# Attention rows ahead of a head's loads, a later wait on TensorE, and an earlier gelu table in a vision transformer layer

## The chip, the cores and the metric

The kernel runs on one core of one Trainium2 chip. The metric is the device time of one execution in microseconds (us). A core has five engines that run side by side and meet at semaphores: TensorE (PE, matrix products), VectorE (DVE), ScalarE (ACT, functions such as exp and gelu), GpSimd (POOL) and SyncE (SP, which only issues transfers here). Each runs its own instructions in order. Products of PE land in PSUM, a memory of eight banks (0 to 7); transfers (DMA) move data between the large memory and the working memory.

## The reference, cut to what matters

```python
h = tok_embed(x)                      # 4 images 224x224, patches of 4: 3137 tokens of 128 features each
h = h + attn(layernorm(h))            # 8 heads of 16, softmax over all 3137 keys
h = h + ffn(layernorm(h))

# attn, for each image and head
attn = softmax(q @ k.T * scale + pos_bias)   # pos_bias from a table of 32 distance buckets
out  = (attn @ v) ... @ Wo

# ffn, for each image
aw     = softmax(x @ attn_w + attn_b)        # over the tokens
pooled = sum(x * aw)                         # one vector
gates  = softmax(pooled @ gate_w + gate_b)   # 8 experts, the best 2 are taken, g is normalised
eo     = gelu(gelu(x @ w1[e] + b1[e]) @ w2[e] + b2[e])   # 128 -> 512 -> 128
y      = g[e1] * eo[e1] + g[e2] * eo[e2]
```

All of it is in float32.

## The kernel before, in words

Tokens lie along the free dimension, features along the 128 partitions. An image (batch b of 4) is cut into 8 chunks of 393 columns (W). There are three parts. The first (to about 212 us) embeds the patches, normalises and computes q, k and v for all images; these go out to the large memory. The second is attention: 32 heads (NBH = 4 x 8), one after the other, and within each head two passes, each over 25 tiles of 128 keys and 4 chunks of queries. The third, from about 2496 us on, is the MLP of the experts.

**Attention.** A unit is one tile of 128 keys by one chunk of queries. `fast_order` puts three units in a group (two where a guest comes in). For a group PE computes scores into three PSUM banks (`scores`, lines 666 and 669), in turn banks 0 to 2 and 3 to 5; ACT takes the exponential of the whole group in one instruction (line 843); POOL multiplies the units near the diagonal by a bias (line 925); PE multiplies by the values four units at a time into banks 6 and 7 (`values`, line 748). PE runs `AHEAD` = 2 groups ahead of ACT. After a pass (25 batches of four units) DVE drains banks 6 and 7 (`drain`, lines 1002 to 1013; the semaphore `s_o` counts the drained passes), normalises, and SP stores the half head to `att_rows` (`store_half`, line 469). A head's q, k and v pieces are eleven transfers (`load_head`, lines 446 and 458), two heads ahead of their use, into the buffers of the head that was just drained, so SP waits for `s_o` first.

**Guests.** While the heads of image b+1 run, PE visits 33 guest matmuls that finish image b's attention and prepare its MLP (`guest_order`, `visit`, line 696): Y multiplies the attention rows of a chunk by Wo, M, V and S are mean, variance and pool scores, G the gates. Three are placed in each pass from the second on, at units 35, 58 and 80 of 100. The one that this text speaks of most, Y4 (the Y of chunk 4), is the second of the fifth pass of a stage; a stage is the 16 passes of one image. The attention rows of chunk c lie in one of four slots, c % 4 of the tile `att`, which shares its memory with `halves` (so a profile calls the load `halves<-att_rows`). Chunks 0 to 3 are loaded at the end of the stage before (line 574), chunks 4 and 5 in the loop of the second head of the stage, 6 and 7 in that of the third. Each `load_attention` first waits until the guest that used the slot before is received (Y0 for chunk 4). The 33 guests of the last image come in the MLP, after unit 3 and each further unit (`LATE`), into bank 6 (`LATE_PS`), one of the two banks that the drain reads.

**SP's order.** SP works through one list in order; for head n: store the first half (which waits for its normalisation), wait until head n's two passes are drained, issue the eleven pieces of head n+2, then the attention rows where there are any, then store the second half.

**The MLP.** A unit U is one chunk and one expert: four products of 128 by 393 into banks 0 to 3 (`experts`, line 712), gelu on ACT (line 861), four products accumulated in bank 4 or 5 (line 720) for the unit before, gelu again (line 868), and DVE adds it to the result (line 1130). Every product is two passes of float32 in the trace (x8 for four products). ACT holds one table of functions at a time; exp and gelu are in different ones, and the builder puts a table load before the first instruction that needs another.

Of the kernel before, what the change touches and what calls it, by code (L numbers as in the profile page):

```python
# [13 lines left out]
ACT = mybir.ActivationFunctionType  # L14
AX_X = mybir.AxisListType.X

P = 128
# [43 lines left out]
def at(count):  # L61

    return count + 1
# [52 lines left out]
def build(nc, B, S, d):  # L116
    T, W, TP, KT = sizes(B, S)
    LAST = T - (KT - 1) * P
    NBH = B * HEADS
# [24 lines left out]
    with top:  # L144
        def sbuf(ctx, name, shape, dt=F32):
            return ctx.enter_context(nc.sbuf_tensor(name, shape, dt))

        def semaphore(ctx, name):
            return ctx.enter_context(nc.semaphore(name))

        held = ExitStack()
# [4 lines left out]
        def primed(ctx, name=None, start=1):  # L156

            s = semaphore(ctx, name) if ctx else spare.pop()  # L160
            to_prime.append((s, start))
            return s
# [9 lines left out]
        eps_t = sbuf(top, "eps_t", [P, 1])  # L172
# [5 lines left out]
        ctx = ExitStack()  # L178
        with ctx:
# [117 lines left out]
            gate_b = sbuf(ctx, "gate_b", [P, E])  # L297
            iota8 = sbuf(ctx, "iota8", [P, 2, E])
            root = sbuf(ctx, "root", [P, 3, W])
            st = sbuf(ctx, "st", [P, B, 16])  # L300
            pooled = sbuf(ctx, "pooled", [P, P])
            gt = sbuf(ctx, "gt", [P, B, 8, E])
# [27 lines left out]
            s_o = primed(held, "f_o")  # L330
# [5 lines left out]
            s_o_out = [primed(held, f"f_o_out{i}") for i in range(2)]  # L336

            s_w3 = semaphore(held, "f_w3")
            s_set3 = semaphore(held, "f_set3")
            s_att = [semaphore(held, f"f_att{i}") for i in range(4)]  # L340
            s_guest_mm = semaphore(held, "f_guest_mm")
# [39 lines left out]
            def guest_number(b, kind, c):  # L381

                return b * GUESTS + guest_list.index((kind, c))

            def expert_unit(U):

                return U // NU, U % NU // 2, U % 2

            LATE = {3 + i: (B - 1) * GUESTS + i for i in range(4 * CH)}
# [47 lines left out]
            def _(sp):  # L437
# [24 lines left out]
                def load_head(n):  # L462
                    for i in range(PIECES):
                        load_piece(n, i)

                def store_half(n, side):
                    sp.wait_ge(s_norm_o, 2 * n + side + 1)
                    dst = bass.AP(att_rows, n * (CH * 32 * W) + side * (4 * 32 * W), [[W, P], [1, W]])
                    sp.dma_start(dst, o_norm[:, side]).then_inc(s_o_out[side], 16)
# [55 lines left out]
                def load_attention(b, c):  # L525

                    if c >= 4:
                        sp.wait_ge(s_guest, guest_number(b, "Y", c - 4) + 1)
                    elif b > 0:
                        sp.wait_ge(s_guest, guest_number(b - 1, "Y", c + 4) + 1)  # L530
                    head = CH * 32 * W
                    src = bass.AP(att_rows, b * (HEADS * head) + c * 32 * W, [[head, HEADS], [W, HD], [1, W]])
                    sp.dma_start(att[:, c % 4], src).then_inc(s_att[c % 4], 16)
# [12 lines left out]
                def load_ln(b):  # L546

                    sp.wait_ge(s_ln2_out[b], 16)
                    sp.dma_start(ln2[b], ln2_rows.ap()[b]).then_inc(s_ln2_in[b], 16)

                for n in range(NBH):
                    b, into = n // HEADS - 1, n % HEADS
                    store_half(n, 0)
                    if n + 2 < NBH:
                        sp.wait_ge(s_o, at(2 * n + 2))
                        load_head(n + 2)
                    if b >= 0 and into == 1:
                        load_attention(b, 4)
                        load_attention(b, 5)
                    if b >= 0 and into == 2:  # L560
                        load_attention(b, 6)
                        load_attention(b, 7)
                    if b >= 0 and into == 6:
                        sp.wait_ge(s_ln2, (b + 1) * CH)
                        sp.dma_start(ln2_rows.ap()[b], ln[:]).then_inc(s_ln2_out[b], 16)
                    if n == NBH - 1:
                        sp.wait_ge(s_pooled, B - 1)
                        sp.wait_ge(s_ln2_out[B - 2], 16)
                        load_ln(0)
                        load_experts(0)  # L570
                    store_half(n, 1)
                    if into == HEADS - 1:
                        for side in range(2):
                            sp.wait_ge(s_o_out[side], at(16 * (n + 1)))
                        for c in range(4):
                            load_attention(b + 1, c)
# [12 lines left out]
            def _(pe):  # L589
# [108 lines left out]
                def experts(U):  # L698

                    if U < B * NU:  # L700
                        b, c, e = expert_unit(U)
                        if U % NU == 0:
                            pe.wait_ge(s_ew[b], EW)
                            if b < B - 1:
                                pe.wait_ge(s_ln2_in[b], 16)
                            else:
                                pe.wait_ge(s_ln2, B * CH)
                        for half in range(2):
                            pe.wait_ge(s_hid, at(max(2 * U + half - 1, 0)))
                            for i in range(2):  # L710
                                sl = 2 * half + i
                                last = nc.tensor.matmul(ps[:, HID_PS + sl, 0:W], w1[b % 2][:, e, sl * P:(sl + 1) * P],  # L712
                                                        ln2[b][:, c * W:(c + 1) * W], start=True, stop=True)
                            last.then_inc(s_hid_mm, 1)
                    if U >= 1:
                        b, c, e = expert_unit(U - 1)
                        pe.wait_ge(s_hid, at(2 * U))
                        pe.wait_ge(s_eo, at(max(U - 2, 0)))
                        for sl in range(HS):
                            last = nc.tensor.matmul(ps[:, EO_PS + U % 2, 0:W], w2[b % 2][:, e, sl], hid[:, (U - 1) % 2, sl],  # L720
                                                    start=(sl == 0), stop=(sl == HS - 1))
                        last.then_inc(s_eo_mm, 1)
# [46 lines left out]
                while done < NB:  # L769
                    values(done)  # L770
                    done += 1
                pe.wait_ge(s_o, at(2 * NBH))
                pe.wait_ge(s_exp, NG)
                pe.wait_ge(s_guest, (B - 1) * GUESTS)
                for U in range(B * NU + 1):
                    experts(U)
                    if U in LATE:
                        visit(LATE[U], LATE_PS)

            @blk.scalar  # L780
            def _(act):
# [48 lines left out]
                def gate_exp(b):  # L830

                    act.wait_ge(s_lg, b + 1)
                    nc.scalar.activation(gt[:, b, 1], gt[:, b, 0], ACT.Exp, bias=st[:, b, 6:7], accum_out=st[:, b, 7:8]).then_inc(s_ge, 1)
# [3 lines left out]
                for g in range(NG):  # L837
# [9 lines left out]
                    if g in gate_exp_at:  # L847
                        gate_exp(gate_exp_at[g])

                for U in range(B * NU + 1):  # L850
                    if U < B * NU:
                        b, c, e = expert_unit(U)
                        if U % NU == 0:
                            act.wait_ge(s_ew[b], EW)
                        if U >= 2:
                            act.wait_ge(s_eo_mm, U - 1)
                        for half in range(2):
                            act.wait_ge(s_hid_mm, 2 * U + half + 1)
                            for i in range(2):
                                sl = 2 * half + i  # L860
                                last = nc.scalar.activation(hid[:, U % 2, sl], ps[:, HID_PS + sl, 0:W], ACT.Gelu,  # L861
                                                            bias=b1[:, 2 * (b % 2) + e, sl:sl + 1])
                            last.then_inc(s_hid, 1)
                    if U >= 1:
                        b, c, e = expert_unit(U - 1)
                        act.wait_ge(s_eo_mm, U)
                        act.wait_ge(s_acc, at(max(U - 2, 0)))
                        nc.scalar.activation(eo[:, (U - 1) % 2], ps[:, EO_PS + U % 2, 0:W], ACT.Gelu,  # L868
                                             bias=b2[:, 2 * (b % 2) + e:2 * (b % 2) + e + 1]).then_inc(s_eo, 1)
                    if U == LATE_EXP:  # L870
                        pool_exp(B - 1)
                    if U == LATE_GEXP:
                        gate_exp(B - 1)
# [267 lines left out]
        ctx = ExitStack()  # L1141
        with ctx:
# [76 lines left out]
            s_o = [primed(ctx, f"s_o{i}") for i in range(2)]  # L1219
# [394 lines left out]
        ctx = ExitStack()  # L1614
# [442 lines left out]
```

## Time and profile before

| | us |
|---|---|
| median of three runs | 2893.42 (2885.08 to 2893.7) |
| the profiled execution, its own time | 2888.52 |
| its span in the trace | 2886.8 |
| ACT busy | 2564.7 (89%) |
| PE busy | 2550.3 (88%) |
| exponentials of line 843, busy / idle before | 2247.2 / 36.0 |

The span is that of the instructions in the trace, and some 1.7 us of the execution's own time lie around it. PE's busy time counts overlapping matmuls once; its share near ACT's doesn't make it a second bound. Idle time of an engine is put down to what ended it.

### The profile page before, as it was taken

The page shows a single profiled execution, that of the slowest core. Times are in us where ns is not written, and L with a number is a line of the kernel's source. Part 1 is how long each engine was busy: PE and PEld are TensorE (multiplying, and loading weights), DVE is VectorE, ACT ScalarE, POOL GpSimd, SP SyncE. Part 2 cuts the span into 40 slices and gives each one's busy share as a digit, 9 for nine tenths or more (in the row PEclk, how much of TensorE's full clock was granted, in tenths as well). Part 3 has the DMA queues.
Part 4 walks back from the last instruction along what each step waited for, and adds up shares of the span by engine and source line. Part 5 has one row for each costly group of instructions (what it writes and reads, how often), then busy time and mean ns, then how long its engine had stood idle before and what let it go on. Part 6 is the DMA issues. An engine that isn't in the chain of part 4 may idle for free.

```text
span 2886.8 us, 121986 instructions
## 1 busy us (share of the span) xinstructions
PE 2550.3 (88%) x55860; PEld 1222.1 (42%) x55860; DVE 846.4 (29%) x1246; ACT 2564.7 (89%) x2732; POOL 785.5 (27%) x1424
## 2 busy tenths in 40 slices
PE   7988888888898999888989998889899988899997
PEld 3443333333343444433434444334344443455554
DVE  5751111111113333211233342112333421244410
ACT  4769999999998999999989999999899999744553
POOL 2113333333323333333333333332333333100000
PEclk9989999999999999999999999999999999999999
DMA  5540111010011110011111100111110000301010
GB/s 136 178 163 11 33 35 31 31 31 30 30 40 34 30 32 30 29 48 32 40 34 32 32 29 29 50 33 37 34 32 31 29 29 31 118 28 32 17 34 19
DMA packets 65896, 125.29 MB, mean 43 GB/s; under 512 B 10034, under 2 KB 55180, under 8 KB 63892
## 3 DMA queue, kind: packets, MB, share of 16 engines
q1 hardware_dynamic: 63324, 110.93, 12.2%
q8 instruction: 444, 7.27, 1.1%
q0 software_dynamic: 2048, 6.43, 0.6%
q14 instruction: 80, 0.66, 0.1%
HBM read 67.30 MB, written 51.30 MB: 41 GB/s over the span
## 4 chain that ended last, share of the span: by engine, by line
ACT 49%; PE 25%; issue 19%; DMA 4%; DVE 1%; SPq 1%; POOL 1%; ACTq 0%; POOLq 0%
ACT shared L843 48%; PE ps L712 6%; PE ps L720 6%; PE ps L748 5%; PE ps L669 3%; PE ps L666 2%; DMA halves<-att_rows 2%; PE ps L696 1%; DMA k_halves<-halves 1%; DVE std L964 1%; POOL ln L911 1%; DMA ln_rows<-ln 0%; PE ps L610 0%; SPq L458 0%; DMA band_rows<-band_sb 0%
## 5 line engine op out<-in xcount | busy, mean ns | idle before, releaser
L843 ACT ACTIVATE shared<-ps 128x1179 f32<-128x1179 f32 x2167 | 2247.2, 1297 | 36.0 <-PE ps L666 28.3
L748 PE MATMUL ps<-shared,va 64*32 64x393 f32 x25600 | 1577.2, 500 | 1.8 <-issue 1.1
L925 POOL TENSOR_TENSOR shared<-shared,e_all 128x310 f32<-128x310 f32 (+19 forms) x1344 | 727.4, 554 | 1571.5 <-ACT shared L843 1565.0
L669 PE MATMUL ps<-qa,ka 48*32 48x393 f16 (+2 forms) x15200 | 728.5, 319 | 149.3 <-ACT shared L843 148.3
L666 PE MATMUL ps<-qa,ka 51*32 51x393 f16 (+8 forms) x13184 | 659.2, 315 | 104.2 <-ACT shared L843 103.7
L748 PEld LDWEIGHTS ps<-shared,va 64*32 64x32 f32 x25600 | 620.8, 139 | 32.7 <-issue 6.6
L669 PEld LDWEIGHTS ps<-qa,ka 48*32 48x32 f16 x15200 | 230.5, 90 | 630.5 <-ACT shared L843 618.4
L666 PEld LDWEIGHTS ps<-qa,ka 51*32 51x32 f16 x13184 | 208.0, 89 | 662.4 <-ACT shared L843 653.4
L1002 DVE COPY xc<-ps 128x393 f32<-128x393 f32 x64 | 36.4, 569 | 1105.5 <-PE ps L748 1105.5
L861 ACT ACTIVATE qa<-ps,b 128x393 f32<-128x393 f32 x256 | 136.4, 586 | 82.2 <-PE ps L712 82.2
L1010 DVE RECIPROCAL sq<-sq 128x393 f32<-128x393 f32 x64 | 167.3, 2615 | 2.2
L868 ACT ACTIVATE ka<-ps,b 128x393 f32<-128x393 f32 x64 | 37.8, 590 | 98.3 <-PE ps L720 98.3
L930 POOL DMA_DIRECT2D out<-h_all x32 | 17.9, 560 | 354.8 <-DVE h_all L1130 354.8
L1130 DVE SCALAR_TENSOR_TENSOR h_all<-ka,gsc,h_all 128x393 f32<-128x393 f32 x64 | 40.2, 628 | 243.3 <-ACT ka L868 243.3
L964 DVE RECIPROCAL std<-std 128x393 f32<-128x393 f32 x32 | 83.7, 2615 | 32.5 <-ACT std L790 32.5
L720 PE MATMUL ps<-qa,v_sb 128*128 128x393 f32 x256 | 89.9, 493 | 0.0
L720 PE MATMUL ps<-qa,e_all 128*128 128x393 f32 x256 | 89.7, 493 | 0.0
L712 PE MATMUL ps<-shared,e_all 128*128 128x393 f32 x256 | 89.7, 493 | 0.0
L911 POOL TENSOR_TENSOR ln<-xc,std 128x393 f32<-128x393 f32 x32 | 32.6, 1017 | 156.4 <-DVE std L964 123.1
L800 ACT ACTIVATE qk_sq<-ps 128x786 bf16<-128x786 f32 x32 | 26.4, 826 | 51.1 <-PE ps L610 28.6
L1022 DVE TENSOR_TENSOR h_all<-h_all,ps 128x393 f32<-128x393 f32 x32 | 18.0, 563 | 162.4 <-PE ps L696 162.4
L720 PEld LDWEIGHTS ps<-qa,e_all 128*128 128x128 f32 x256 | 48.6, 190 | 36.1
(141 smaller groups left out, 1344.8 us busy)
## 6 DMA issues: line engine op xcount, KB each, us to landing
qa<-q_halves SPq DMA_DIRECT2D x64, 196.5 KB
ka<-k_halves SPq DMA_DIRECT2D x64, 196.5 KB
att_rows<-std SPq DMA_DIRECT2D x64, 196.5 KB, 3.2
v_rows<-v_sb SPq DMA_DIRECT2D x4, 1600.0 KB, 6.8
va<-v_rows SPq DMA_DIRECT2D x32, 200.0 KB, 16.0
ln_rows<-ln SPq DMA_DIRECT2D x32, 196.5 KB, 5.7
q_halves<-halves SPq DMA_DIRECT2D x32, 196.5 KB, 3.0
k_halves<-halves SPq DMA_DIRECT2D x32, 196.5 KB, 4.4
```

The lines of the kernel that those rows point to most:

```text
L666: last = nc.tensor.matmul(out[x:y, 0:cut], ka[r:r + 51, par, k0 + x:k0 + y], qa[r:r + 51, par, q0:q0 + cut], start=True, stop=True, tile_p ...
L669: last = nc.tensor.matmul(out[x:y, cut:W], ka[r:r + 48, par, k0 + x:k0 + y], qa[r:r + 48, par, q0 + cut:q0 + W], start=True, stop=True, ti ...
L712: last = nc.tensor.matmul(ps[:, HID_PS + sl, 0:W], w1[b % 2][:, e, sl * P:(sl + 1) * P], ln2[b][:, c * W:(c + 1) * W], start=True, stop=True)
L720: last = nc.tensor.matmul(ps[:, EO_PS + U % 2, 0:W], w2[b % 2][:, e, sl], hid[:, (U - 1) % 2, sl], start=(sl == 0), stop=(sl == HS - 1))
L748: last = nc.tensor.matmul(ps[quad:quad + 32, O_PS + half, 0:W], va[r:r + 64, par, :, kt], pr[r:r + 64, g % SLOTS_PR, j], start=(kt == 0), ...
L843: nc.scalar.activation(pr[:, g % SLOTS_PR, 0:m], ps[:, b0:b0 + m, 0:W], ACT.Exp, scale=1.0 / (LIFT * LIFT)).then_inc(s_exp, 1)
L861: last = nc.scalar.activation(hid[:, U % 2, sl], ps[:, HID_PS + sl, 0:W], ACT.Gelu, bias=b1[:, 2 * (b % 2) + e, sl:sl + 1])
L911: nc.gpsimd.tensor_tensor(ln[:, columns(c)], xc[:, c % 2], std[:, c % 2], ALU.mult).then_inc(s_ln, 1)
L925: nc.gpsimd.tensor_tensor(p, p, e_all[0:keys, n % HEADS, t:t + z - a], ALU.mult).then_inc(s_biased, 1)
L964: nc.vector.reciprocal(std[:, c % 2], std[:, c % 2]).then_inc(s_rstd, 1)
L1010: nc.vector.reciprocal(inv[:, side], inv[:, side]).then_inc(s_inv, 1)
L1130: nc.vector.scalar_tensor_tensor(h, eo[:, (U - 1) % 2], gsc[:, b, e:e + 1], h, ALU.mult, ALU.add).then_inc(s_acc, 1)
```

## The change

Three edits. SP issues the attention rows of chunks 4 and 5 (second head of a stage) and of chunks 6 and 7 (third head) before it waits for the drained head and loads the head after next, no longer behind that. PE no longer waits for the last drain before the first expert unit but before the first late guest, after the matmuls of unit 3 (`min(LATE)`). ACT applies gelu to one column behind its last exponential, into a tile `warm` that nothing reads; `s_warm` is waited for by nobody.

```diff
+            warm = sbuf(ctx, "warm", [P, 1])
...
+            s_warm = semaphore(held, "f_warm")
...
                     store_half(n, 0)
-                    if n + 2 < NBH:
-                        sp.wait_ge(s_o, at(2 * n + 2))
-                        load_head(n + 2)
                     if b >= 0 and into == 1:
                         load_attention(b, 4)
                         load_attention(b, 5)
                     if b >= 0 and into == 2:
                         load_attention(b, 6)
                         load_attention(b, 7)
+                    if n + 2 < NBH:
+                        sp.wait_ge(s_o, at(2 * n + 2))
+                        load_head(n + 2)
...
-                pe.wait_ge(s_o, at(2 * NBH))
                 pe.wait_ge(s_exp, NG)
                 pe.wait_ge(s_guest, (B - 1) * GUESTS)
                 for U in range(B * NU + 1):
                     experts(U)
+                    if U == min(LATE):
+                        pe.wait_ge(s_o, at(2 * NBH))
                     if U in LATE:
                         visit(LATE[U], LATE_PS)
...
+                nc.scalar.activation(warm[:], eps_t[:], ACT.Gelu).then_inc(s_warm, 1)
                 for U in range(B * NU + 1):
```

## Rows read from the trace of the kernel before

**Rows 1.** The page, part 1: busy us, share of the span and instructions
```profile
PE 2550.3 (88%) x55860; PEld 1222.1 (42%) x55860; DVE 846.4 (29%) x1246; ACT 2564.7 (89%) x2732; POOL 785.5 (27%) x1424
```
**Rows 2.** Groups of ACT instructions: count, busy us, mean ns, idle before and releaser
```profile
L843 ACT ACTIVATE shared<-ps 128x1179 f32<-128x1179 f32 x2167 | 2247.2, 1297 | 36.0 <-PE ps L666 28.3 <-PE ps L669 6.3
...
L861 ACT ACT_TABLE_LOAD x3 | 3.8, 1283 | 4.6 <-PE ps L712 4.6
```
**Rows 3.** Timeline of ACT from 1012 us: start, us, what, [idle before <-releaser]
```profile
1011.01 19.77 ACT L843 ACTIVATE shared<-ps 128x1179 f32<-128x1179 f32 x19
```
**Rows 4.** The chain of waits, first piece of this kind: start, us, what
```profile
918.49 16.50 DMA halves<-att_rows
```
**Rows 5.** Timeline of SP's issues, first stage with guests
```profile
847.99 33.67 SPq L469 DMA_DIRECT2D att_rows<-std  x2
912.45 1.07 SPq L458 DMA_DIRECT2D qa<-q_halves  x2
...
918.49 4.71 SPq L533 DMA_DIRECT2D halves<-att_rows  x2
```
**Rows 6.** Timeline of all engines, 925 to 942 us
```profile
924.25 5.03 ACT L843 ACTIVATE shared<-ps 128x1179 f32<-128x1179 f32 x5
...
935.04 1.68 PE L696 MATMUL ps<-halves,wo 128*128 128x393 f32 x2 [7.12 <-DMA halves<-att_rows]
...
937.54 1.15 ACT L843 ACTIVATE shared<-ps 128x1179 f32<-128x1179 f32 x1 [8.27 <-PE ps L666]
...
939.21 1.16 ACT L843 ACTIVATE shared<-ps 128x1179 f32<-128x1179 f32 x1 [0.52 <-PE ps L666]
...
941.15 1.15 ACT L843 ACTIVATE shared<-ps 128x1179 f32<-128x1179 f32 x1 [0.78 <-PE ps L666]
```
**Rows 7.** Windows: from:to, us, busy of each engine, granted clock, DMA share, GB/s
```profile
930.85:941.09 10.24, 6.05 (x78) 2.83 (x86) 0.57 (x1) 2.31 (x2) 0.00 (x0) 0.50 0.07 26
...
941.09:1228.00 286.91, 259.01 (x6920) 121.75 (x6902) 100.13 (x150) 286.60 (x279) 92.94 (x168) 1.00 0.10 31
```
**Rows 8.** Windows of two passes each, from drain to drain
```profile
880.70:960.34 79.64, 65.95 (x1687) 30.76 (x1679) 23.05 (x33) 70.01 (x69) 25.13 (x42) 0.94 0.10 31
...
1102.19:1172.00 69.81, 63.06 (x1687) 29.86 (x1679) 34.24 (x54) 69.75 (x69) 23.23 (x42) 1.00 0.10 30
```
**Rows 9.** Timeline of ACT behind the other two stalls
```profile
1513.39 1.16 ACT L843 ACTIVATE shared<-ps 128x1179 f32<-128x1179 f32 x1 [8.32 <-PE ps L666]
1514.91 5.33 ACT L843 ACTIVATE shared<-ps 128x1179 f32<-128x1179 f32 x5 [0.36 <-PE ps L666]
...
2089.94 1.15 ACT L843 ACTIVATE shared<-ps 128x1179 f32<-128x1179 f32 x1 [9.00 <-PE ps L666]
...
2091.61 9.30 ACT L843 ACTIVATE shared<-ps 128x1179 f32<-128x1179 f32 x9 [0.52 <-PE ps L666]
```
**Rows 10.** Timeline of DVE: the second guest of the stage, Y1, is received
```profile
822.95 0.56 DVE L1022 TENSOR_TENSOR h_all<-h_all,ps 128x393 f32<-128x393 f32 x1 [7.60 <-PE ps L696]
```
**Rows 11.** Windows, with DMA share and GB/s last: the MLP's first transfers
```profile
2505.00:2510.00 5.00, 5.00 (x16) 2.85 (x15) 0.00 (x0) 2.45 (x6) 0.00 (x0) 1.00 0.32 101
```
**Rows 12.** Timeline of PE, ACT and SP at the end of attention
```profile
2500.23 2.91 PE L712 MATMUL ps<-ln,v_sb 128*128 128x393 f32 x8 [1.25 <-DVE xc L1005]
...
2501.90 1.28 ACT L861 ACT_TABLE_LOAD   x1 [4.56 <-PE ps L712]
2503.20 2.03 ACT L861 ACTIVATE qa<-ps,b 128x393 f32<-128x393 f32 x4
...
2504.32 2.91 PE L712 MATMUL ps<-ln,v_sb 128*128 128x393 f32 x8 [1.18 <-ACT qa L861]
...
2506.41 2.72 SPq L533 DMA_DIRECT2D halves<-att_rows  x4
...
2520.28 0.82 PE L696 MATMUL ps<-halves,wo 128*128 128x393 f32 x2
```
**Rows 13.** Groups of PE instructions from 2497 us on: the first image's units
```profile
L712 PE MATMUL ps<-ln,v_sb 128*128 128x393 f32 x128 | 45.1, 494 | 2.4 <-DVE xc L1005 1.2 <-ACT qa L861 1.2
```

## The prediction

> **What bounds the kernel now.** I read the page's engine table first. ScalarE (ACT) is busy 89% of a span of 2886.8 us, TensorE (PE) 88% [rows 1]. Two engines at almost the same share say little, so the second view was the groups of ACT instructions. The 2167 exponentials of line 843 are 2247.2 us of busy time with 36.0 us of idle time ahead of them in total [rows 2]. So in attention (about 212 to 2496 us) ACT is the bound. 19 exponentials in a row take 19.77 us where nothing disturbs them, about 1.045 us from one start to the next [rows 3]. Of the 36.0 us of idle time 28.3 are put down to the short score matmuls of line 666, which can't be the bound by themselves. The third view, the chain of waits, names what stands behind them: "DMA halves<-att_rows", in three pieces of which the first is 16.50 us long and the others, one stage later each, 16.07 and 16.14 [rows 4]. After 2496 us the MLP of the experts starts, and there the chain is PE, unit after unit.
>
> **The three stalls.** In each of three stages (batches 1 to 3, in which batch b-1 gets its late work) PE visits guest matmul Y4 and finds its attention rows not there. SP issues those rows only behind the eleven pieces of load_head: the wait for the drained head ends at 912.4, the pieces are issued from 912.45 on, the rows at 918.49 [rows 5], and they land 16.50 us later, at 934.99 [rows 4]. PE reached the guest near 927.9 and resumes at 935.04. Two groups of scores are kept ahead, so ACT has something to do until 929.28, and then idles 8.27 us [rows 6].
>
> What one stall costs, read from ACT's starts. Stage 1: idle 8.27, and the next exponentials start at 937.54, 939.21 and 941.15, so 1.67 and 1.94 us apart where 1.045 is the rule: 0.63 + 0.89 more [rows 6]. PE's clock is at half by then (0.50 from 930.85 to 941.09, its lower level of 1.2 GHz, after it had stood still) [rows 7]. Together 9.8. A check without single instructions: from the drain at 880.70 to the one at 960.34 two passes took 79.6 us; the stretch from 1102.19 to 1172.00, also between two drains and with the same 69 ACT instructions, took 69.8 [rows 8]. The difference is 9.8 again. Stage 2: 8.32 + (1.52 - 1.045) = 8.8. Stage 3: 9.00 + (1.67 - 1.045) = 9.6 [rows 9]. The sum is 28.2 us.
>
> **Part 1, rows ahead of the next head.** Nothing is added; the two loads of 196 KB are issued right after the first store of the head, ahead of the wait. In stage 1 that store follows the drain of 880.70, so they start at about 881.7. Their own condition is that the guests Y0 and Y1 are received, the later one at 822.95 [rows 10], so SP doesn't stop there. Issuing takes 4.7 us as before [rows 5], until 886.4, and SP is then at the wait for the drained head, which ends at 912.4: the eleven pieces are issued when they were before. The second store of the head gets 4.7 us earlier, which no one needs. Even with a landing as slow as today's 16.5 us the rows are there at 898, 29 us ahead of the guest. With no head in front of them they are faster: at the start of the MLP four such loads are issued from 2506.41 on, behind a store of the same 196 KB, and 505 KB were moved until 2510 (101 GB/s for 5 us) [rows 11, 12], which is the store and one and a half of the loads, so about 4 us for the first. What is late next at the same place? The rows of Y5 come with those of Y4 and are wanted more than a pass later. Those of Y6 and Y7 move in the same way one head later; no wait of PE stands on them today (three waits on these rows are all there are, one a stage). What is then uncovered is ACT's ordinary 1.045 us a group. So the gain is the whole 28.2 us. Bounds: 25.1 by the idle time alone (8.27 + 8.32 + 9.00 = 25.6, less 0.5 should the guest cost ACT something by itself) and 30.5, should low stretches of the clock elsewhere go too.
>
> A side term: 36.0 us of idle time less that of the stalls and right behind them (25.6, and 0.52, 0.78, 0.36, 0.52) leaves 8.2 us elsewhere [rows 2, 6, 9]. Some of it, a few us in the whole kernel, follows the three pool exponentials, behind which PE's clock falls as well, and how much depends on where the fall lands. All of these move by 10 to 28 us, so they are dealt anew: plus or minus 1.5 us, nothing on average.
>
> **Part 2, the wait for the last drain.** Before: the first expert matmul starts at 2500.23, behind 1.25 us of idle time that the drain ends [rows 12], so PE was done with the values at 2498.98. Now it goes on at once, at about 2499.03: the banks of the experts' products are not those that the drain reads. The wait stands before the guest of unit 3, which PE reached at 2520.28 [rows 12]; the drain has been over for 20 us by then, and behind the wait are queued only that guest and unit 4, so it costs nothing. The drain and the store after it stay at their times. The first late rows are issued at 2506.41 [rows 12] and by the estimate above are there at about 2510; the guest now comes at 2517.9. The rows bound the landing only by 2520.28, where PE did not wait; were it as late as that, the gain here would be 2.4 us smaller.
>
> **Part 3, the table of gelu.** Before: ACT loads it at 2501.90 for 1.28 us after 4.56 us of idle time, the first gelu starts at 2503.20, and PE waits 1.18 us for it before unit 1, which starts at 2504.32 [rows 12]. Now one gelu of one column sits behind the last exponential, in those idle 4.56 us. Load and gelu take 1.28 plus at most 0.6 us (four gelus of 393 columns take 2.03 [rows 12]), over before 2499.3. Nothing waits behind them until PE's first products at 2500.7. Without that cover they would cost up to 1.9 us.
>
> Parts 2 and 3 together: ACT can start 1.67 us after PE (2501.90 - 2500.23), at 2500.7; half of the 2.03 us for four gelus, until 2501.75; PE itself is through with unit 0 at 2499.03 + 2.91 = 2501.94, and starts unit 1 then. Before it was 2504.32: 2.4 us. From there PE shows no other wait for batch 0's weights: the 2.4 us of the two gaps are all the idle time of that group of 128 matmuls [rows 13], so everything behind moves by the gain. Bounds: 1.2 (the wait alone, if the gap in front of unit 1 stays) and 2.7.
>
> ScalarE's load shows as 1.283 us, with 0.02 us between it and the gelu [rows 2, 12]. The Trainium skill (ScalarE: Activation LUTs, What ACT_TABLE_LOAD costs) adds a drain of about 1.38 us, 2.66 us for a switch. By it load and gelu would end 1.4 us later, by 2500.7 and so just in time: the same 2.4 us. This trace has no second piece behind the load; a drain could only lie in the idle 4.56 us ahead of it.
>
> **Sum.** 28.2 + 2.4 = 30.6 us. The profiled execution took 2888.5 us, so 2857.9 on its footing. The median of the three runs, 2893.4, is 4.9 above that execution, and 2893.4 - 30.6 = 2862.8. I take 2861, between the two.
>
> **Rivals.**
> - A: the stall goes only in part, because the landing stays slow or a later Y waits in turn. For it: in stage 1 the head's pieces and the rows were in flight together, and only one order has been seen. Against it: 29 us of slack at today's slowest landing. If half of ACT's idle time stayed (12.8 us) the time would be 2893.4 - 30.6 + 12.8 = 2875.6.
> - B: the transition gives nothing, for example since a unit further on waits for gelu instead. Then the time is 2861 + 2.4 = 2863.4. Against: PE shows only two gaps there [rows 13]. It lies inside the range.
> - C, the slower side: TensorE does not keep its full clock through a longer stretch. Today's stalls cut attention into stretches at 1.00, one of them 287 us long [rows 7]; without them such a stretch gets about twice as long. If the clock fell to its lower level in it, groups would come 0.63 to 0.89 us late each, as behind the stall [rows 6]. From 34 to 49 such groups in the whole kernel on, the gain is eaten; with 60 groups at 0.76 the time is 2893.4 - 30.6 + 46 = 2909. Against it: in these rows the clock fell only after PE had idled.
> - D: the order of issue had no part in it, so only Parts 2 and 3 are left: 2891.0, no change that can be told. Against: SP's wait for the head ended at 912.4 and the other condition at 822.95 [rows 5, 10]; nothing but the order kept the rows back.
>
> **How the numbers follow.** The forecast 0.80, B 0.06, A 0.07, C 0.03, D 0.03, and 0.01 for what I don't see. About 0.3%, 8.7 us, is what a measurement of this kernel can tell from no change. Faster by more: forecast, B, A and the rest, 0.94. Within: D, 0.03. Slower: C, 0.03. The range: gains of 25.1 + 1.2 - 1.5 = 24.8 to 30.5 + 2.7 + 1.5 = 34.7 us, from runs of before between 2885.1 and 2893.7, end at 2850.4 and 2868.9. One us more above, towards A, gives 2850 to 2870.
>
> **What would show it.** In the profile after: idle time ahead of line 843 near 10 us instead of 36.0; no "halves<-att_rows" in the chain; SP's rows right behind the first store of the second head of a stage and ahead of its wait; the clock without a low stretch at Y4; a table load and a small gelu on ACT before PE's first expert products; PE without a gap before units 0 and 1. The forecast is wrong if PE still waits some us in front of a guest, if line 843's groups come more than 1.05 us apart over a long stretch, or if unit 1 starts more than 3.2 us after the last values.

## The result and the profile after

| | before | changed |
|---|---|---|
| median of 4 runs, us | 2892.11 (2885.08 to 2893.7) | 2858.59 (2854.74 to 2861.5) |
| ratio, 95% interval | | 0.9888 [0.9867, 0.9909] |
| span of the profiled execution | 2886.8 | 2859.8 |
| first exponential of line 843 starts | 206.4 | 211.0 |
| attention: from there to the end of the last one | 2290.9 | 2260.0 |
| end of the last exponential to the start of unit 1 on PE | 6.97 | 4.38 |

The change makes the kernel 33.5 us faster by these medians. The forecast was 2861 in a range of 2850 to 2870, and a gain of 30.6. In a second series, beside the other experiments, the same kernel had 2859.87 against 2889.35, 29.5 us (0.9895 [0.9879, 0.9912]).

The groups of ACT instructions after the change (line 846 is line 843 of before):
```profile
L846 ACT ACTIVATE shared<-ps 128x1179 f32<-128x1179 f32 x2167 | 2246.4, 1302 | 5.9 <-PE ps L671 4.3
```
The busy time is nearly that of [rows 2], the idle time ahead of it has gone from 36.0 to 5.9 us. SP's issues in the first stage with guests:
```profile
885.87 0.34 SPq L471 DMA_DIRECT2D att_rows<-std  x1
886.26 1.37 SPq L535 DMA_DIRECT2D halves<-att_rows  x2
917.01 1.10 SPq L460 DMA_DIRECT2D qa<-q_halves  x2
```
The rows leave right behind the first store, 30.7 us before the next head's first piece; in [rows 5] they left 6.0 us behind it. Their issue takes 1.4 us and not 4.7. At the guest, ACT and PE (timeline):
```profile
927.77 22.69 ACT L846 ACTIVATE shared<-ps 128x1179 f32<-128x1179 f32 x22
...
932.42 0.93 PE L698 MATMUL ps<-halves,wo 128*128 128x393 f32 x2
```
There is no wait ahead of the guest's matmul, and 22 exponentials follow one another over it. The windows say the same: first the two passes with Y4, from drain to drain as in [rows 8] (to within 0.1 us), then the longest stretch at full clock:
```profile
885.28:955.05 69.77, 63.01 (x1685) 29.79 (x1677) 22.97 (x33) 69.69 (x69) 25.05 (x42) 1.00 0.12 35
...
222.00:1228.90 1006.90, 890.50 (x24278) 405.59 (x24270) 222.91 (x326) 1006.38 (x969) 321.50 (x599) 1.00 0.10 31
```
79.64 us have become 69.77, as in the undisturbed 69.81, and PE's clock is full for 1006.9 us without a break. The end of attention:
```profile
2467.17 3.80 ACT L846 ACTIVATE shared<-ps 128x1179 f32<-128x1179 f32 x4
...
2470.99 1.28 ACT L853 ACT_TABLE_LOAD   x1
...
2472.28 0.20 ACT L853 ACTIVATE warm<-eps_t 128x1 f32<-128x1 f32 x1
2472.54 2.28 PEld L714 LDWEIGHTS ps<-ln,v_sb 128*128 128x128 f32 x8 [0.61 <-issue]
2472.64 0.57 DVE L1006 COPY xc<-ps 128x393 f32<-128x393 f32 x1 [26.14 <-PE ps L750]
...
2474.23 1.07 ACT L865 ACTIVATE qa<-ps,b 128x393 f32<-128x393 f32 x2 [1.74 <-PE ps L714]
2475.35 0.96 PEld L714 LDWEIGHTS ps<-ln,v_sb 128*128 128x128 f32 x4 [0.53 <-ACT qa L865]
```
The drain (line 1006) runs beside the first expert matmuls, which start at 2472.54, and gelu follows PE's first products after 1.7 us with no load in between; unit 1 starts at 2475.35. In [rows 12] the same steps took until 2504.32, with a gap before each.

### The profile page after: what moved, and what is told of

Read it like the earlier page. It is cut to its first block, busy times and chain, and to the rows that moved or that the text cites. A ratio compares the mean times of both kernels' runs of the same rounds, so it can differ in the third digit from the quotient of the medians.

```text
span 2859.8 us, 121986 instructions
## 1 busy us (share of the span) xinstructions
PE 2547.9 (89%) x55860; PEld 1222.0 (43%) x55860; DVE 846.0 (30%) x1246; ACT 2564.2 (90%) x2733; POOL 786.6 (28%) x1424
## 4 chain that ended last, share of the span: by engine, by line
ACT 51%; PE 26%; issue 19%; DMA 2%; DVE 1%; POOL 0%; SPq 0%; ACTq 0%; POOLq 0%
ACT shared L846 50%; PE ps L714 6%; PE ps L722 6%; PE ps L750 5%; PE ps L671 3%; PE ps L668 2%; PE ps L698 1%; DMA k_halves<-halves 1%; PE ps L612 1%; PE ps L606 1%; PE ps L627 0%; DMA band_rows<-band_sb 0%; DVE std L968 0%; POOL ln L915 0%; PE ps L620 0%
## 5 line engine op out<-in xcount | busy, mean ns | idle before, releaser
L668 PEld LDWEIGHTS ps<-qa,ka 51*32 51x32 f16 x13184 | 205.8, 89 | 660.6 <-ACT shared L846 658.7
L722 PEld LDWEIGHTS ps<-qa,v_sb 128*128 128x128 f32 x256 | 48.9, 191 | 36.6 <-issue 1.0
L722 PEld LDWEIGHTS ps<-qa,e_all 128*128 128x128 f32 x256 | 48.6, 190 | 36.1
```

Source lines behind the costliest of these rows:

```text
L668: last = nc.tensor.matmul(out[x:y, 0:cut], ka[r:r + 51, par, k0 + x:k0 + y], qa[r:r + 51, par, q0:q0 + cut], start=True, stop=True, tile_p ...
```

## The experiments

In all of them "idle" is the idle time ahead of the exponentials of attention, and "to unit 1" the time from the end of the last one to the start of unit 1 on PE. The times of before, changed, e1, v1 and v2 are medians of four or more runs, all others are one run; the last four columns come from one profiled execution each.

| kernel | time | first exp. | attention | idle | to unit 1 |
|---|---|---|---|---|---|
| before | 2889 to 2892 | 206.4 | 2290.9 | 36.0 | 6.97 |
| changed | 2858.6 | 211.0 | 2260.0 | 5.9 | 4.38 |
| e1 rows only | 2863.2 (0.9902 [0.9879, 0.9925]) | 211.8 | 2259.9 | 6.0 | 6.97 |
| e2 wait only | 2892.6 | 212.6 | 2289.6 | 35.1 | 5.66 |
| e3 table only | 2891.1 | 210.3 | 2289.4 | 34.9 | 5.69 |
| e4 wait and table | 2886.1 | 204.7 | 2290.9 | 36.1 | 4.38 |
| e5 rows behind SP's wait | 2866.3 | 211.7 | 2262.4 | 8.1 | 6.98 |
| e6 rows behind five pieces | 2859.5 | 205.8 | 2260.8 | 6.6 | 6.97 |
| e7 pieces split | 2899.0 | 194.6 | 2312.4 | 53.6 | 6.98 |
| e8 only chunks 4 and 5 | 2859.4 | 205.3 | 2261.1 | 7.0 | 6.97 |
| e9 split and paced | 2846.7 | 194.4 | 2260.7 | 6.7 | 6.97 |
| v1 earlier maximum | 2853.9 (0.9871 [0.9854, 0.9887]) | 209.4 | 2260.4 | 6.4 | 4.38 |
| v2 all together | 2840.2 (0.9829 [0.9815, 0.9842]) | 194.2 | 2261.4 | 7.4 | 4.38 |

The first exponential moves by up to 8 us between executions whose first part is the same (all but e7, e9 and v2). That is the noise of a single run, so attention and "to unit 1" are compared, not single times.

### The parts by themselves

**e1, the rows only** (the middle block of the diff above).

> Only the attention rows are issued ahead of the wait and of the next head's pieces. If the eleven pieces in front were the whole cause, the three stalls go: idle time ahead of line 843 from 36.0 to below 10 us, attention (first exponential to end of the last) from 2290.9 to some 2260 us, the time 28 to 31 us below before. Rival (the landing stays slow, or a later guest waits in its turn): idle time of 15 us or more, and a wait of PE for att_rows further on.

28.7 us faster, attention 31.0 us shorter, as in the changed kernel. The rows make all of attention's gain. No wait of PE for att_rows is left in its trace.

**e2, the wait only.**
```diff
-                pe.wait_ge(s_o, at(2 * NBH))
...
+                    if U == min(LATE):
+                        pe.wait_ge(s_o, at(2 * NBH))
```


> Only PE's wait for the last drain is moved to unit 3. From the end of the last exponential to the start of unit 1 on PE before needs 6.97 us. If the table load stays as long as it is and now follows PE's first products, 5.8 us: a gain of 1.2 of the 2.6 that the changed kernel shows. Rival (the drain's wait was covered by the table load anyway): 6.9 us, no gain. The three stalls stay: about 28 us of idle time ahead of line 843.

6.97 to 5.66, 1.3 us. PE starts unit 0 1.57 us behind the last exponential and no longer 2.89, and the gap of 1.18 us before unit 1 stays, behind the table load. Timeline of e2:
```profile
2505.35 1.28 ACT L862 ACT_TABLE_LOAD   x1 [3.24 <-PE ps L712]
...
2507.77 0.60 PE L712 MATMUL ps<-ln,v_sb 128*128 128x393 f32 x1 [1.18 <-ACT qa L862]
```

**e3, the table only** (the line with `warm`).

> Only the gelu table is loaded behind the last exponential. End of the last exponential to the start of unit 1: 6.97 us before. If the load is on the path, 5.7 to 5.8 us (PE's own 2.9 us for unit 0 then follow the drain). Rival (load and wait hide each other, each alone gives nothing): 6.9 us. The three stalls stay.

6.97 to 5.69, again 1.3 us: unit 0 still starts 2.89 us behind the last exponential, and the gap before unit 1 is gone.

**e4, both.**

> Before with Parts 2 and 3, rows as they were. End of the last exponential to the start of unit 1: 4.4 us as in the changed kernel, 2.6 less than before, the sum of the two alone. Stalls stay at about 28 us of idle time ahead of line 843. Rival (what follows the stalls decides the transition): another value than 4.4.

4.38, 2.59 less: 1.31 and 1.28 add up. The two edits shorten pieces of one chain that lie one behind the other; neither hid the other.

### Why the rows were late

**e5, the rows behind SP's wait, ahead of the pieces.**
```diff
                     if n + 2 < NBH:
                         sp.wait_ge(s_o, at(2 * n + 2))
-                        load_head(n + 2)
                     if b >= 0 and into == 1:
                         load_attention(b, 4)
...
+                    if n + 2 < NBH:
+                        load_head(n + 2)
```


> Before, with the rows issued behind SP's wait for the drained head but ahead of all eleven pieces of the next head. If the pieces in front make the landing slow, the rows issued near 912.5 land 4 to 6 us later, 10 us ahead of the guest, and no stall is left: idle time ahead of line 843 below 10 us. Rival (it is the late issue behind the wait, with the transfers of pieces and rows sharing the engines whatever their order): the rows land 12 to 20 us after the wait's end, and a stall of 1 to 4 us a stage stays.

No stall is left. SP's wait for the drained head has no part in it; the pieces have.

**e6, the rows behind five of the eleven pieces.**
```diff
-                        load_head(n + 2)
+                        for i in range(5):
+                            load_piece(n + 2, i)
...
+                        for i in range(5, PIECES):
+                            load_piece(n + 2, i)
```


> Before, with the rows issued behind five of the eleven pieces. If the landing grows with what is queued in front (16.5 us behind eleven, some 4 behind none), the rows issued near 915.5 land 9 to 11 us later, near 926, and PE, which is at the guest near 928, just doesn't wait or waits under 1 us. Rival (only the issue's time counts, every landing 16 us): landing near 931.5, idle time of 3 to 4 us a stage on ACT.

No stall either. The rows' semaphore is complete at 925.5, 11.0 us behind their issue at 914.4. None in front: 3.8 us in e5, 4.7 in the changed kernel. Five in front: 11. Eleven: 16.5 [rows 4]. So what is queued in front sets the landing. Not every part of the rows is late, though. A transfer raises its semaphore step by step as its parts are done, here in nine steps: seven of them had come by 918.3, the last two at 925.35 and 925.46.

**What is slow in the pieces.** A window of before, in the middle of the stall:
```profile
929.00:934.80 5.80, 0.00 (x0) 0.00 (x0) 0.00 (x0) 0.27 (x1) 0.00 (x0) 0.66 0.13 50
```
The DMA share is 0.13 at 50 GB/s, which is what two busy engines of sixteen would give (2/16 = 0.125). The four pieces that fill 32 partitions have a leading dimension of two (`[[0, 2], [TP, HD], [1, TP]]`). The rows' semaphore had seven of its nine steps 5.4 us behind their issue (918.5 to 923.9) and the last two at 934.8 and 935.0: most of the rows had landed, and two parts were late, as if they stood in the queues of two engines. The Trainium skill (DMA: Bandwidth & Descriptors, Rules for kernel authors) says that a leading dimension of c below 16 confines a transfer to at most c engines. This row agrees with it.

**e7, the four pieces split.**
```diff
-                    par, half, what = n % 2, i // 5, i % 5
+                    par, half, what = n % 2, i // 7, i % 7
...
-                        dst, src = qa[r:r + 2 * HD, par], bass.AP(q_halves, head, [[0, 2], [TP, HD], [1, TP]])
+                        dst, src = qa[r:r + HD, par], bass.AP(q_halves, head, [[TP, HD], [1, TP]])
...
+                    elif what == 5:
+                        dst, src = qa[r + HD:r + 2 * HD, par], bass.AP(q_halves, head, [[TP, HD], [1, TP]])
...
-                PIECES = 11
+                PIECES = 15
```
(k's pieces in the same way, and 14 in place of 10 transfers that a head's semaphore counts.)

> Before, order as it was, but each of the four pieces that fill 32 partitions with a leading dimension of two (q's high half twice, k's high and low half) is issued as two transfers of 16 rows: fifteen pieces in place of eleven, the same bytes. In the trace of before the DMA share stands near 0.12, two engines of sixteen, for the last 10 us before the rows land. Theory: those pieces lie on two engines, whose queues the rows then share; split, all is there earlier, the rows (issued some 2 to 3 us later than before) land 5 to 8 us behind their issue, near 927, and the stalls shrink to under 1.5 us a stage: idle time ahead of line 843 (its new number aside) 6 to 12 us in place of 36. Rival (the bytes of the head, 1.4 MB, have to go first, whatever engines carry them): landing 16 us after the issue, idle time of 36 to 44 us.

The theory held for the landing and failed for the idle time; its rival failed in the landing. The rows did land fast, 7.5 us behind their issue (922.4 to 929.9), in the order of before and with the same bytes in front, and PE never waits for them; so the two engines were the cause of the 16.5 us. But idle time rose to 53.6 us and the time to 2899.0. PE's waits in attention (us in total, times, longest):
```profile
PE ps L670 <- issue: 21.7, 21, 4.0
PE ps L752 <- issue: 15.1, 14, 3.9
```
Before has one such wait there, of 1.1 us. The longest one of e7, for which ACT then waits 4.03 us, and a window of 10 us ahead of it:
```profile
1508.69 0.84 PE L670 MATMUL ps<-qa,ka 51*32 51x393 f16 x12 [4.00 <-issue]
```
```profile
1491.00:1501.00 10.00, 9.35 (x259) 4.42 (x254) 4.37 (x5) 9.53 (x10) 5.26 (x11) 1.00 0.94 122
```
PE stands for 4.0 us, waiting for nothing that the profile shows, and ACT runs dry behind it. Ahead of it the DMA share is 0.94; in before at the same work it is 0.35:
```profile
1488.00:1498.00 10.00, 9.48 (x271) 4.51 (x265) 4.56 (x7) 9.99 (x11) 5.47 (x11) 1.00 0.35 93
```
The page's queue table has 7.27 MB on a queue of kind "instruction", in 444 packets. The reading I took from that: PE's code comes through the same sixteen engines and stands behind a head's 1.4 MB when all of them are full.

The trace of e7 bears this out. A packet of that queue has 16384 bytes, and the trace has 113108 instructions of PE, so some 64 bytes of code for each, or 256 to a packet. In attention PE has 37 issue waits, 38.3 us in total. Each one ends 1.2 to 1.9 us behind the end of such a packet. And in each PE stands at the same count: it has started 449 of its instructions more than 256 times the packets that had come before that one. It is the same 449 at the single issue wait that before, the changed kernel and e9 have in attention. Nowhere in the attention of these four traces does it get further ahead. So PE had run out of code. The packet that ends the wait of 4.0 us takes 1.04 us itself, no more than the others (1.1 us in the median); it starts late, at 1506.1, when the share has just fallen: 0.88 from 1498.3 to 1506.1, 0.21 in the 1.1 us behind it.

**e9, the split pieces in pairs**, with the rows ahead as in the changed kernel.
```diff
                     for i in range(PIECES):
                         load_piece(n, i)
+                        if i % 2 == 1:
+                            sp.wait_ge(s_ld[n % 2], (n // 2) * (NLD * 16) + 16 * (i + 1))
```


> The changed order of the rows with the fifteen split pieces, and SP waits for every pair of them to land before it issues the next. The kernel with split pieces alone had no wait of PE for att_rows (rows issued at 922.4, used without a stall) and yet 53.6 us of idle time ahead of the exponentials, ended by PE that itself had waited for nothing shown (issue), at or right behind a head's load, where the DMA share is 0.9 to 1.0 over 10 us. Theory (PE's instructions come through the same sixteen engines and stand behind a head's transfers): paced, the share stays below 0.6, the issue waits of PE in attention go back to a few us, idle time ahead of the exponentials 6 to 15 us, attention 2260 to 2268 us. Rival (the smaller transfers, 16 rows each, cost the same however they are spread in time, by their writes to the tiles that PE reads): 35 to 55 us of idle time.

Same transfers, spread over 22 us: the DMA share is 0.21, and the issue waits are back to one of 1.2 us.
```profile
829.00:852.00 23.00, 20.52 (x552) 9.79 (x552) 6.19 (x10) 22.99 (x24) 8.63 (x17) 1.00 0.21 57
```
So it isn't the smaller transfers but their density. e9 differs from e7 in the place of the rows too, but that can't be the reason: all but one of e7's issue waits come 6 to 18 us behind the start of a head's load, at 27 of the 30 loads, and only six loads have rows beside them. What stays open is at which point full engines hold a packet of code up.

What I had not expected is the first part. The first exponential starts at 194.4 us, at 194.6 in e7 and at 194.2 in v2 below, where the eleven traces with the wide pieces have 204.7 to 212.6. Heads 0 and 1 are loaded in that part, between the stores of the halves, and ACT's wait for those stores falls with the split. Waits of ACT in before, then in e9:
```profile
ACT qk_sq L800 <- DMA k_halves<-halves: 22.5, 7, 7.5
```
```profile
ACT qk_sq L806 <- DMA k_halves<-halves: 6.5, 1, 6.5
```

**e8, only chunks 4 and 5 moved.**

> Before, with only the rows of chunks 4 and 5 moved ahead; those of chunks 6 and 7 stay behind the third head's pieces. Theory (only Y4's rows were late): idle time ahead of line 843 near 6 us, attention near 2260 us as with all four moved. Rival (with the first stall gone the rows of Y6 or Y7 are late in their turn): a wait of PE for att_rows of 1 to 8 us a stage.

Attention 2261.1, no wait for att_rows. The move of chunks 6 and 7 brings nothing that this run shows.

### Versions beyond the change

**The changed kernel again, and v1, the last maximum one unit earlier.**
```diff
-            LATE_MAX, LATE_EXP, ... = 36, 36, 37, 39, 39, 40
+            LATE_MAX, LATE_EXP, ... = 35, 36, 37, 39, 39, 40
...
                     if U == LATE_MAX:
+                        dve.wait_ge(s_guest, B * GUESTS - 1)
                         pool_max(B - 1)
```


> The changed kernel once more, as the one that the version with the earlier maximum is held against. By its first runs it is 0.9888 of before; 0.988 to 0.990 expected, so 28 to 35 us.

> The changed kernel, with the maximum over the last image's pool scores taken by DVE one unit earlier (behind unit 35's addition, and a wait for the last score guest, which is there by then). In the changed kernel ACT waits 2.91 us for that maximum with exp's table loaded, PE is idle 4.99 us before unit 38 and its clock is low for 6.8 us after it. Theory: the 2.9 us go, the gap in front of unit 38 is 2 to 2.2 us, the clock stays up or is low for 3.4 us only, so 3 to 5 us less than the changed kernel. Rival (DVE is late with the additions and holds ACT at the following unit): the gap moves to unit 37 and the time is the same.

2853.89 (2849.16 to 2856.03) against 2859.87 (2856.64 to 2861.76) in the same series. From the end of attention to the end of the program 384.5 in place of 388.4 us. PE before unit 38, in the changed kernel and in v1:
```profile
2697.32 5.61 PE L714 MATMUL ps<-shared,v_sb 128*128 128x393 f32 x8 [4.99 <-ACT qa L865]
```
```profile
2693.24 4.27 PE L714 MATMUL ps<-shared,v_sb 128*128 128x393 f32 x7 [2.09 <-ACT qa L865]
```
The gap shrinks by 2.9 us, and the clock behind it is low for 3.4 us and not for 6.8. These 3.8 us are what the two traces show; the other 2 us between the medians lie in neither.

**v2, all together**: the changed kernel with e7's split, e9's pairs and v1's maximum.

> All that helped together: the changed kernel, the fifteen split pieces issued in pairs that SP waits for, and the last image's maximum one unit earlier. By the parts: first part until the first exponential near 194.5 us (206 to 212 before; the paced kernel 194.4), attention 2260 to 2261 us, from its end to the end of the program 384.5 us. Sum 2839 to 2840 of span, 2841 us of time, 0.982 to 0.984 of before. Rival (the parts get in each other's way, by PE's instruction loads for instance): 2846 us or more.

2840.24 (2838.67 to 2845.13), 0.9829 of before [0.9815, 0.9842], so 51 us below before and some 18 below the changed kernel. Its parts are 194.2, 2261.4 and 382.9. It is faster than both kernels.

## Why the prediction was right, step by step

**The number.** A gain of 30.6 us was forecast; the two series gave 33.5 and 29.5, and the two traces give 30.9 + 2.6 = 33.5 for the stretches that the change touches. That the time itself, 2861 against 2858.6, came out so near is in part luck: the forecast was put between two footings 4.9 us apart, and the two series differ by 4.0 us in their gain.

**Part 1.** Right in mechanism and nearly in size. 28.2 us were forecast for the three stalls. The check by two passes gives 79.64 - 69.77 = 9.9 for stage 1 (9.8 forecast). Attention shortened by 30.9 (31.0 in e1), 2.7 more than the stalls. So it lies just above the bound of 30.5 that I gave for this part. Two of the 2.7 are the side term that I put at "nothing on average", plus or minus 1.5: behind the second and third pool exponential the clock was low for 6.8 us in before and is for 3.4 now. Before, then changed:
```profile
1808.08:1814.91 6.83, 6.19 (x97) 3.44 (x104) 0.00 (x0) 5.53 (x6) 0.00 (x0) 0.50 0.01 2
```
```profile
1795.53:1798.94 3.41, 3.41 (x62) 1.80 (x54) 0.00 (x0) 2.63 (x3) 0.00 (x0) 0.50 0.00 0
```
The excess of the exponentials' starts over 1.045 us behind the three was 0.9, 2.1 and 1.8 us and is 0.5, 1.3 and 1.0. It isn't dealt at random either: e2, e3 and e4, which keep the stalls, show 3.4, 6.8 and 6.8 us of low clock in the three places, and e1, e5, e6, e8 and e9 3.4 in each. Why the second and third get off better once Y4 no longer stalls is open. Another size that was off is the issue of the rows: 1.4 us in place of 4.7, where nothing stood in front of them. "Even with a landing as slow as today's 16.5 us the rows are there" was a safe bound, but the prediction had no account of why that landing was slow; it was the price of pieces that ran on two engines (e6, e7). The 4 us that it gave for a landing with no head in front were 4.7, and 3.8 in e5.

**Part 2 and 3.** 2.4 forecast, 2.59 measured, and each alone the 1.3 that the gaps of 1.25 and 1.18 in [rows 12] said (bound: 1.2). Unit 3's guest came without a wait, so the late wait and the first late rows cost nothing, as reckoned. The load was over at 2472.3, before PE's first expert matmul. The tiny gelu starts 0.01 us behind the load, so the drain of 1.38 us that the Trainium skill (ScalarE: Activation LUTs, What ACT_TABLE_LOAD costs) puts beside it shows nowhere here.

**What was given back.** The spans differ by 27.0 us and not by 33. The first part was 4.6 us longer in this execution, which the change doesn't touch. In the MLP the units of the changed kernel start 28.97 us ahead from unit 1 to unit 38 and 27.60 from unit 39 on: behind the gap before unit 38 the clock was low for 6.8 us in place of 3.4 (5.61 against 4.57 us for the eight matmuls). This isn't the work of the change: of the twelve traces with the old maximum ten have 6.8 us there, among them e2, e3 and e4 with the stalls and e1, e5, e6 and e8 without Parts 2 and 3; only before and e9 have 3.4. The last 0.6 us lie behind the issue of the last transfer.

**The rivals.** A: no wait at Y4 or a later Y; e8 shows that there was none to fear even with 6 and 7 in their old place. B: refuted by 6.97 to 4.38. C: refuted by 1006.9 us at 1.00. The prediction held it against the 287 us of [rows 7] and overlooked that before already had 713.3 us at 1.00 without a break, from 217.5 to 930.8; that alone made this rival weaker than it was put. D: refuted by e1, e5 and e6.

## What to carry to other kernels

A wait that ends on a transfer asks two questions: when was it issued, and what stood in front of it on the same engines. A window over the stall with its DMA share answers the second; 0.13 with a transfer outstanding meant two engines of sixteen here, a matter of the access pattern's leading dimension. And when such transfers are spread over all engines, pace them: here attention of the unpaced version took 52 us more than that of the paced one, with 38 us of PE's issue waits and what followed them, although PE waited for none of these transfers any more.

## What the runs showed of the hardware that I had not expected

- Busy DMA engines starve TensorE of its code: with a share of 0.94 over 10 us PE had issue waits up to 4.0 us (37 of them in attention, 38 us in total), with the same transfers at 0.21 one of 1.2 us. Each ended 1.2 to 1.9 us behind a 16384-byte packet of the instruction queue, with PE at the same count of instructions.
- Four transfers of 196 KB with a leading dimension of two, among eleven, delayed an unrelated transfer behind them to 16.5 us from some 4, and only in two of its nine steps. The first part of this kernel was 10 to 18 us longer with such transfers in it than with each split in two.
- ACT's load of gelu's table follows the last exponential within 0.02 us and takes 1.28 us, with nothing behind it.
